# Last attention block: values as weights, heads written turned, row sums from products with ones

## The reference

```python
def mha(xq, ctx, wq, wk, wv, wo, bo):          # H = 16, DH = 64
    q, k, v = (heads of xq @ wq, ctx @ wk, ctx @ wv)
    scores = jnp.einsum('bhqd,bhkd->bhqk', q, k) / math.sqrt(DH)
    attn = jax.nn.softmax(scores, axis=-1)
    out = jnp.einsum('bhqk,bhkd->bhqd', attn, v)
    return out.transpose(0, 2, 1, 3).reshape(b, sq, INNER) @ wo + bo
# x = x + mha(adaln(x), adaln(x), ...); x = x + mha(adaln(x), context, ...); x = x + glu_ff(adaln(x), ...)
```

## Time and profile before

| | us |
|---|---|
| median of 3 runs | 5407.77 (5390.87 to 5420.82) |
| span of the profiled execution | 5413.8 |
| granted TensorE clock, mean | 0.918 |
| TensorE matmul busy | 4614.7 (85%) |
| VectorE busy | 2884.4 (53%) |
| ScalarE busy | 2082.3 (38%) |
| own attention of the second pass | 4697.4 to 4773.5 |

### The profile page before, as it was taken

The page is one execution under the profiler, slowest core; times in us unless marked ns, Lnnn a source line. Parts: engine busy times, 40 slices in busy tenths (PEclk is TensorE's granted clock), DMA queues, the critical chain, the costliest instruction groups (busy, mean ns, idle before and its releaser), DMA issues. The chain is left out here.

```text
span 5413.8 us, 111310 instructions
## 1 busy us (share of the span) xinstructions
PE 4614.7 (85%) x45206; PEld 3112.5 (57%) x45501; DVE 2884.4 (53%) x9511; ACT 2082.3 (38%) x4120; POOL 576.5 (11%) x1302
## 2 busy tenths in 40 slices
PE   5489999999999965889989889899778979788784
PEld 3357777777777753555555555555444756566463
DVE  6634555555555535777766677666455224433433
ACT  2223333333333312665665666566433322212221
POOL 3300111111111112111111111111000000000000
PEclk8789999999999976999999999999889989878786
DMA  0000000000000011000000000000010010000000
GB/s 26 23 18 2 2 2 2 2 2 2 2 2 2 2 61 54 4 4 6 7 6 4 4 9 4 6 1 1 1 40 1 1 44 1 1 1 1 1 1 9
DMA packets 32272, 49.22 MB, mean 9 GB/s; under 512 B 8244, under 2 KB 23638, under 8 KB 31136
## 3 DMA queue, kind: packets, MB, share of 16 engines
q1 hardware_dynamic: 28448, 38.27, 2.2%
q10 hardware_dynamic: 2304, 2.11, 0.1%
q0 software_dynamic: 1024, 1.78, 0.1%
HBM read 37.72 MB, written 4.19 MB: 8 GB/s over the span
## 5 line engine op out<-in xcount | busy, mean ns | idle before, releaser
L2299 DVE TENSOR_REDUCE l_m<-psum 128x2 bf16<-128x512 f32 x768 | 503.8, 692 | 148.8 <-PE psum L1904 146.5
L2175 ACT ACTIVATE l_probs<-psum,l_mcol 128x1024 f32<-128x1024 f32 x384 | 406.3, 1109 | 159.2 <-PE psum L1942 159.2
L1184 PE MATMUL psum<-g_gx,ident 128*128 128x128 f32 x1536 | 416.0, 389 | 18.0
L1173 PE MATMUL psum<-g_still,ident_bf 128*128 128x256 bf16 (+3 forms) x1551 | 391.5, 281 | 1.7 <-PEq L58 1.7
L1904 PE MATMUL psum<-l_kb,l_qmb 32*128 32x256 bf16 x1536 | 295.4, 273 | 56.1 <-DVE l_m L2299 52.4
L1252 ACT ACTIVATE g_th<-g_pre 128x256 f32<-128x256 f32 x512 | 191.7, 417 | 314.3 <-DVE g_pre L1285 314.3
L1184 PEld LDWEIGHTS psum<-g_gx,ident 128*128 128x128 f32 x1536 | 279.4, 195 | 12.8
L1942 PE MATMUL psum<-l_qm,l_keys 32*128 32x256 f32 x3072 | 265.1, 418 | 13.3 <-issue 13.3
L2186 ACT COPY l_heads_out<-psum 128x256 f32<-128x256 f32 (+1 forms) x292 | 130.0, 445 | 369.8 <-PE psum L1968 186.3
L1285 DVE TENSOR_TENSOR g_pre<-g_encp,psum 128x256 f32<-128x256 f32 x512 | 192.8, 418 | 132.9 <-PE psum L1202 122.4
L2299 DVE TENSOR_REDUCE l_cm<-psum 128x4 bf16<-128x256 f32 x400 | 166.0, 427 | 179.8 <-PE psum L1904 179.6
(11 more groups left out here) (567 smaller groups left out, 9761.9 us busy)
## 6 DMA issues: line engine op xcount, KB each, us to landing
s_w<-in_S_w SPq DMA_DIRECT2D x16, 256.0 KB, 5.0
f_w<-in_F_w SPq DMA_DIRECT2D x2, 2048.0 KB, 12.5
l_wf<-in_L_W SPq DMA_DIRECT2D x6, 576.0 KB, 3.8
l_w<-in_L_W SPq DMA_DIRECT2D x1, 3072.0 KB, 10.6
l_nw<-in_L_nw SPq DMA_DIRECT2D x1, 2304.0 KB, 8.0
l_wc<-in_L_W SPq DMA_DIRECT2D x6, 384.0 KB, 3.0
h_w<-in_H_W ACTq DMA_DIRECT2D x16, 129.0 KB, 3.0
h_w<-in_H_W SPq DMA_DIRECT2D x16, 129.0 KB, 3.0
```

The lines of the kernel that those rows point to most:

```text
L1173: pe.matmul(psum[:, bank, 0:cols], cst["ident_bf"][:], still[:, 0:cols], start=True, stop=True)
L1184: pe.matmul(psum[:, bank, 0:P], cst["ident"][:], repeated(gx(gate, s)), start=True, stop=False)
L2175: act.activation(probs[:, u % 2, chunk, :].rearrange("p (g n) -> p g n", g=GROUP), psum[:, 0:GROUP, S * chunk:S * chunk + S], ACT.Exp, bia ...
L2299: dve.tensor_reduce(place, psum[:, c.bank(("max", u, g)), 0:x.tiles * x.width] .rearrange("p (t k) -> p t k", t=x.tiles), AX.X, ALU.min)\
```

## The change

In `values` the operands trade places: the value columns of a head (64) are the weights and the probabilities (256 queries) stream, so that a head comes out turned, 64 rows for its dimensions and 256 columns for its queries. Two heads fill the 128 rows of a bank's first half. The row sums come from products of a 128 x 64 block of ones with the same probabilities, into the bank's second half, for both key chunks; every one of a head's 64 rows then holds the same sum. The reciprocal covers all of them, and the multiplication writes the turned, normalised heads into `outT`. The transposes, their copies, and their semaphores go, and `project_out` reads `outT`. The column of ones behind the values and its two memsets go too.

```diff
-                        def values(u, t):
+                        def values(u, j):
...
-                            for h in range(GROUP):
-                                for c in range(2):
-                                    last = pe.matmul(psum[:, 6 + t, L3_COLS * h:L3_COLS * (h + 1)],
-                                                     probs[:, u % 2, c, 2 * (h % 2) + h // 2, P * t:P * t + P],
-                                                     v[:, 2 * b + c, GROUP * g + h, :], start=c == 0, stop=c == 1)
+                            for c in range(2):
+                                for i, rows in enumerate(HALVES):
+                                    pe.matmul(psum[rows, 6 + j, 0:S], v[:, 2 * b + c, GROUP * g + 2 * j + i, :],
+                                              probs[:, u % 2, c, 2 * i + j, :], start=c == 0, stop=c == 1)
+                            for c in range(2):
+                                for i, rows in enumerate(HALVES):
+                                    last = pe.matmul(psum[rows, 6 + j, S:2 * S], cst["ones"][:], probs[:, u % 2, c, 2 * i + j, :],
+                                                     start=c == 0, stop=c == 1)
...
-                            for h in range(GROUP):
-                                for b, rows in enumerate(HALVES):
-                                    last = pe.matmul(psum[:, 6 + b, L3_COLS * h:L3_COLS * (h + 1)],
-                                                     probs[rows, u % 2, 0, 2 * (h % 2) + h // 2, P * t:P * t + P],
-                                                     vc[rows, GROUP * u + h, :], start=True, stop=True)
+                            for i, rows in enumerate(HALVES):
+                                for b, keys in enumerate(HALVES):
+                                    pe.matmul(psum[rows, 6 + b, 0:S], vc[keys, GROUP * u + 2 * j + i, :],
+                                              probs[keys, u % 2, 0, 2 * i + j, :], start=True, stop=True)
+                            for i, rows in enumerate(HALVES):
+                                for b, keys in enumerate(HALVES):
+                                    last = pe.matmul(psum[rows, 6 + b, S:2 * S], cst["ones"][keys, :],
+                                                     probs[keys, u % 2, 0, 2 * i + j, :], start=True, stop=True)
...
-                                last = pe.matmul(psum[:, 4 + t, 0:D], qT[:, ch, P * t:P * t + P], wo[:, i, ch, :],
+                                last = pe.matmul(psum[:, 4 + t, 0:D], outT[:, ch, P * t:P * t + P], wo[:, i, ch, :],
...
-                        dve.reciprocal(rsum[:, i % 2, :, :], both[:, :, :, L3_DH]).then_inc(sig[n + "_sums_inverted"], 1)
+                        dve.reciprocal(inverse[:, i % 2, :, :], psum[:, 6:8, S:2 * S]).then_inc(sig[n + "_sums_inverted"], 1)
                         dve.wait_ge(sig[n + "_sums_inverted"], i + 1)
-                        dve.tensor_tensor(dst, both[:, :, :, 0:L3_DH],
-                                          rsum[:, i % 2, :, :].unsqueeze(3).to_broadcast([P, 2, GROUP, L3_DH]), ALU.mult)\
+                        dve.tensor_tensor(dst, psum[:, 6:8, 0:S], inverse[:, i % 2, :, :], ALU.mult)\
                             .then_inc(sig[n + "_values_taken"], 1)
```

More of the change, by code:

```diff
@@ L3133, in glu_block @@
         qb, kb = sb("qb", [P, L3_CH, PTOK], BF16), sb("kb", [P, L3_CH, PTOK], BF16)
-        v, vc = sb("v", [P, PT, H, L3_COLS]), sb("vc", [P, H, L3_COLS])
+        v, vc = sb("v", [P, PT, H, L3_DH]), sb("vc", [P, H, L3_DH])
         m = sb("m", [P, H * 4], BF16)
@@ L3137, in glu_block @@
         probs = sb("probs", [P, 2, 2, GROUP, S])
-        rsum = sb("rsum", [P, 2, 2, GROUP])
-        o = sb("o", [P, PT, H, L3_DH])
+        inverse = sb("inverse", [P, 2, 2, S])
+        outT = sb("outT", [P, L3_CH, PTOK])
         hT = kT[:, 0:L3_FF, :]
@@ L3265, in values @@
                             g, b = divmod(u, 2)
-                            if t == 0:
+                            if j == 0:
                                 pe.wait_ge(sig["self_probs_ready"], 2 * (u + 1))
@@ L3269, in values @@
                                     pe.wait_ge(sig["self_values_taken"], u)
[L3270 to L3275 removed]
+                            for c in range(2):
[6 more added lines that the diff above has]
+                                                     start=c == 0, stop=c == 1)
+                            if j == 1:
                                 last.then_inc(sig["self_values_ready"], 1)
@@ L3330, in scores, with values @@
                             last.then_inc(sig["cross_scores_ready"], 1)
-                        def values(u, t):
+                        def values(u, j):
                             if not 0 <= u < cross_units:
                                 return
-                            if t == 0:
+                            if j == 0:
                                 pe.wait_ge(sig["cross_probs_ready"], u + 1)
-                            if 2 * u + t:
-                                pe.wait_ge(sig["cross_values_taken"], 2 * u + t)
-                            for h in range(GROUP):
-                                for b, rows in enumerate(HALVES):
-                                    last = pe.matmul(psum[:, 6 + b, L3_COLS * h:L3_COLS * (h + 1)],
-                                                     probs[rows, u % 2, 0, 2 * (h % 2) + h // 2, P * t:P * t + P],
-                                                     vc[rows, GROUP * u + h, :], start=True, stop=True)
+                            if 2 * u + j:
+                                pe.wait_ge(sig["cross_values_taken"], 2 * u + j)
+                            for i, rows in enumerate(HALVES):
[6 more added lines that the diff above has]
+                                                     probs[keys, u % 2, 0, 2 * i + j, :], start=True, stop=True)
                             last.then_inc(sig["cross_values_ready"], 1)
@@ L3360, in project_out @@
                     def project_out(n, i, rounds):
-                        def turn(ch):
-                            if ch >= 4:
-                                pe.wait_ge(sig[n + "_outT_ready"], ch - 3)
+                        pe.wait_ge(sig[n + "_values_taken"], rounds)
+                        for ch in range(L3_CH):
                             for t in range(PT):
[L3365 to L3376, removed]
-                                last = pe.matmul(psum[:, 4 + t, 0:D], qT[:, ch, P * t:P * t + P], wo[:, i, ch, :],
+                                last = pe.matmul(psum[:, 4 + t, 0:D], outT[:, ch, P * t:P * t + P], wo[:, i, ch, :],
                                                  start=ch == 0, stop=ch == L3_CH - 1)
@@ L3432, in exponentials @@
                                        ACT.Exp, scale=L3_DH ** -0.5).then_inc(sig[n + "_probs_ready"], 1)
[L3434 to L3439, removed]
                     modulate("n1", 0)
@@ L3450, in _ @@
                         exponentials("cross", u, 0, 2, 2 * (u % 2), u + 1)
-                    turned_out("cross")
                     modulate("n3", 2)
@@ L3487, in normalise @@
                         dve.wait_ge(sig[n + "_values_ready"], i + 1)
-                        both = psum[:, 6:8, 0:GROUP * L3_COLS].rearrange("p t (h e) -> p t h e", e=L3_COLS)
-                        dve.reciprocal(rsum[:, i % 2, :, :], both[:, :, :, L3_DH]).then_inc(sig[n + "_sums_inverted"], 1)
+                        dve.reciprocal(inverse[:, i % 2, :, :], psum[:, 6:8, S:2 * S]).then_inc(sig[n + "_sums_inverted"], 1)
                         dve.wait_ge(sig[n + "_sums_inverted"], i + 1)
-                        dve.tensor_tensor(dst, both[:, :, :, 0:L3_DH],
-                                          rsum[:, i % 2, :, :].unsqueeze(3).to_broadcast([P, 2, GROUP, L3_DH]), ALU.mult)\
+                        dve.tensor_tensor(dst, psum[:, 6:8, 0:S], inverse[:, i % 2, :, :], ALU.mult)\
                             .then_inc(sig[n + "_values_taken"], 1)
[L3495 to L3499, removed]
                     def residual(n, products, i):
@@ L3518, in _ @@
                             g, b = divmod(u - 1, 2)
-                            normalise("self", u - 1, o[:, 2 * b:2 * b + 2, GROUP * g:GROUP * g + GROUP, :])
-                    turned_out("self")
+                            normalise("self", u - 1, outT[:, 2 * g:2 * g + 2, S * b:S * b + S])
                     residual("self_projected", psum[:, 4:8, 0:D], 0)
@@ L3530, in _ @@
                             if u >= 1 and h % 2:
-                                t = h // 2
-                                normalise("cross", 2 * (u - 1) + t, o[:, t:PT:2, GROUP * (u - 1):GROUP * u, :])
-                    turned_out("cross")
+                                ch = 2 * (u - 1) + h // 2
+                                normalise("cross", ch, outT[:, ch, :].rearrange("p (b s) -> p b s", b=2))
                     residual("cross_projected", psum[:, 4:8, 0:D], 1)
```

3 lines of the change are left out of this document (removed).

## The result

| | before | changed |
|---|---|---|
| median | 5414.3 us (5390.9 to 5434.8, 4 runs) | 5614.5 us (5612.1 to 5619.7, 4 runs) |
| ratio to before | | 1.0364, interval [1.0324, 1.0403] |
| span of the profiled execution | 5413.8 | 5614.6 |
| granted clock, mean | 0.918 | 0.903 |
| the block, first to last product | 871.9 | 1065.8 |

The account below looks back on a forecast made before the run. It took own attention to be bound by a chain on TensorE with VectorE close beside it; 21.4 + 8 + 21.0 - 6.5 = 43.9 us a pass, 176 for four, gave 5583 us, range 5505 to 5658.

Parts of the forecast that it names:

- The reciprocal: On VectorE, widening from 8 to 512 columns takes 3.35 us, 3.14 more, from a line through narrower widths.
- Rival 1: The wide reciprocal streams like the multiplication, 0.69 us, giving 5399 us, no change that can be told; chance 0.07.
- `values` in 1.86 us, two side by side: In own attention a call's 16 records overlap in pairs on TensorE, 0.07 us less than before.
- Rival 2: The halves don't run side by side, so 16 calls of 1.6 us more give 5687 us; chance 0.07.
- Own attention, waits, +21.4: TensorE waits for VectorE behind the wide reciprocal, 2.8 us in units 2 to 6; +21.4 us a pass.
- The clock, +8: Seven new waits in own attention invite half-clock stretches, 1.1 us each; +8 us a pass, 0 to 18.
- Rival 3: The clock holds in own attention and rises in cross attention, -8 and -7 us a pass, 5523 us; chance 0.14.
- Cross attention, +21.0: Eight values calls, each tied to the normalisation before it, 6.15 us each; stage 50.4 against 29.4 us.
- Projection, -6.5: Turning and copies go; 9.7 us, starting at half clock, against 13.8 and 12.3; -6.5 us a pass for both.
- Sum: All terms together: 43.9 us a pass, 176 us for four passes, so the runs should show 5583 us.
- The range's low end: Clock holding and rising as above with a projection at full clock: 106 us more, 5505 with some scatter.

Follow-up runs that it names:

- e1: Changed kernel with the reciprocal covering only 8 columns of the sums, the rest of the inverse constant at one, so output isn't normalised; 5356.1 us.
- e6: Changed kernel with the loops over halves and key chunks exchanged in own attention's values, so neighbouring products write the same half; 5609.9 us.
- e5: Changed kernel with unused bfloat16 products on TensorE in own attention's waits, ten ahead of the waiting scores, sixteen before the last values; 5577.6 us.
- e10: Changed kernel with the wide reciprocal and its multiplication moved between the first and second row maximum in VectorE's queue, own attention only; 5573.2 us.
- e7: Kernel before with a spare 512-column reciprocal ahead of each narrow one, and own attention's TensorE waits filled with unused bfloat16 products; 5595.2 us.

## Why the prediction was right, and which terms were off

- **The reciprocal** (3.35 us, 3.14 more): 3358 ns. The line through 4 and 16 columns held to 512. Rival 1 is out. e1 shows that this one size decides the sign.
- **`values` in 1.86 us, two side by side**: 1.88, from 4769.18 to 4771.06 in the second pass. Rival 2 is out; that the halves are the reason isn't shown, since e6 pairs its records too.
- **Own attention, waits, +21.4**: TensorE waited 2.74 us for the row maximum in five units, 2.35 in unit 7, and 4.28 and 4.18 where it had waited 1.12 and 1.03, so 13.7 + 2.35 + 3.16 + 3.15 = 22.4, and less 16 calls shorter by 0.05 it is 21.6.
- **The clock, +8** (0 to 18): the second pass grew by 28.2, so 6.6 are left for it. Rival 3 is out: behind the wait that ends at 4780.15 the granted clock was 0.56 for 6.8 us, behind the one that ends at 4818.45 it was 1.00 for 10.6, and e5 gives 9 us back when it doesn't fall.
- **Cross attention, +21.0, was mis-sized.** The calls came 6.2 us apart for the 6.15 worked out. But the pass that I followed in the trace of before (39.8 us) was the slowest of its four; the others took 31.4 and 36.1. From their mean of 35.9 the stage grew by 24.3, so the term was 3.3 a pass too small, 13 us in all. The changed kernel's stage takes the same 60.2 in every pass, most of it the way through VectorE. I had left it at half clock, as TensorE would be idle for most of it. That held in all four passes, but it was in part luck: in some passes of e5, e6 and e10, with the same code for the stage, the clock was higher and it took 56.3 or 56.4, about half of the 7 us that rival 3 put on it.
- **Projection, -6.5**: with 9.97 and 10.34 us instead of 9.7 for the 64 records, -3.6 and -2.1, or -5.7. It starts at half clock behind a wait of 4.2 us; behind the short waits of e1 the 12.1 us to the next stage are 2.4 less.
- **Sum**: 28.8 + 24.3 - 3.6 - 2.1 = 47.4 a pass against 43.9, 190 against 176. The four stages of the second pass alone, from which the terms came, grew by 43.0. The rest of the block took 4 us more and what lies outside the block, which nothing changed, some 7 between the two profiles; no run says why, and 7 is less than the scatter of the runs of before. The forecast of 5583 us lay 32 under the 5614.5 measured, inside its range.
- **The range's low end** was put at 4 x (43.9 - 15 - 2.3) = 106 us over the runs of before. The 2.3 us that a projection gains at full clock stand in it once, where a pass has two; with both it is 97, and 5407.8 + 97 is the 5505 that it names without its allowance for scatter.

## What to carry to other kernels

Before a per-column statistic is turned into a full tile, price its slow operation at the new width: a reciprocal of 8 columns took 0.21 us here, and the one of 512 in its place cost 258 us in all, more than four times what the rest of the change gained. When a term is taken from one pass of a loop, look at the other passes first. And where an engine stands in a wait, ask what stands behind the waiting instruction in each queue, and what the clock does afterwards.

## What the runs showed of the hardware

- VectorE's reciprocal took 178 ns for 4 columns, 207 for 8, 253 for 16 and 3353 (from SBUF) or 3358 (from PSUM) for 512: nearly a straight line of 6.25 ns a column, with no row between 16 and 512.
- Sixteen f32 records of 256 columns and 64 output rows took 1.88 us, 0.12 for each, with neighbours on different halves, and 1.93 with neighbours on the same half (e6).
- The wide reciprocal cost the two forms of the kernel differently. The granted clock of own attention was 0.88 in the changed kernel and 0.57 in the kernel before with the spare one added, 104.4 against 130.9 us. Why it comes back in the one and not in the other stays open; with filled waits both run at 0.98 and take 95.4 and 96.3.
- Ten unused products in a wait gained time: 9 us a pass in e5, 34 in e7.
- Logarithm and exponential of 128x512 take 0.60 and 0.63 us with one table loaded ahead of the stage: an inverse in 1.3 us on ScalarE, from the start of the one to the end of the other, beside 3.36 on VectorE.
